# A residual stream turned so that tokens lie on the partitions, in a recurrent and windowed-attention kernel

## The reference, cut to what matters

```python
def ref(x, ...):                                   # x: (8, 256, 128), 8 batches of 256 tokens
    xn = layernorm(x)                              # over the 128 features
    s = recurrence(xn)                             # u = gelu(..)*sigmoid(..); s_t = s_(t-1) A' + u_t B'; y = s C' + D
    h = xn
    for i in range(6):
        h = attn_layer(shift_tokens(h), ...) + h   # q, k, v of 16 heads of 64; l2norm, rotary, window 32, softmax, @ Wo
        h = ffn_layer(shift_tokens(h), ...) + h
    return x + s * silu(h)

def shift_tokens(t):                               # half of the features come from the token before
    a, s = jnp.split(t, 2, -1)
    s = jnp.pad(s, ((0, 0), (1, 0), (0, 0)))[:, :-1]
    return jnp.concatenate([a, s], -1)

def ffn_layer(x, g, bln, W1, b1, W2, b2):
    mu = x.mean(-1, keepdims=True)
    var = ((x - mu) ** 2).mean(-1, keepdims=True)
    xn = (x - mu) / jnp.sqrt(var + 1e-05) * g + bln
    a, gate = jnp.split(xn @ W1 + b1, 2, -1)       # 341 columns each
    return a * jax.nn.gelu(gate, approximate=False) @ W2 + b2
```

## Time and profile before

| | |
|---|---|
| median of 3 runs | 1746.93 us (1746.70 to 1748.54) |
| profiled execution | 1748.49 us, span 1746.7 us |
| PE busy | 1695.2 us (97%), 30558 matmuls |
| PEld | 1198.8 us (69%) |
| DVE | 1391.6 us (80%) |
| ACT | 1232.3 us (71%) |
| POOL | 1129.3 us (65%) |
| share of PE in the chain that ended last | 94% |
| mean granted TensorE clock | 0.991 |

### The profile page before, as it was taken

One profiled execution on the slowest core, in us unless ns is written; L12 is line 12 of the kernel. 1 busy time (PEld: TensorE's weight loads), 2 busy tenths in 40 slices (PEclk: granted clock), 3 DMA queues, 4 the chain that ended last, 5 costly groups with the idle time before them and its releaser, 6 DMA issues.

```text
span 1746.7 us, 72189 instructions
## 1 busy us (share of the span) xinstructions
PE 1695.2 (97%) x30558; PEld 1198.8 (69%) x30558; DVE 1391.6 (80%) x2607; ACT 1232.3 (71%) x2173; POOL 1129.3 (65%) x1066
## 2 busy tenths in 40 slices
PE   5889999999999999999999999999999999999996
PEld 2356777777777777777777777777777777777774
DVE  4688888888888888888888888888888888888762
ACT  2256777777777677777777777777777777777763
POOL 0477676667766766776676676667766666776640
PEclk9799999999999999999999999999999999999998
DMA  3133223323222332222323322322322332322222
GB/s 106 24 93 69 61 57 75 84 70 71 66 59 73 86 75 59 71 61 61 89 66 80 71 60 60 86 70 71 77 63 56 75 88 70 71 63 59 59 56 73
DMA packets 82830, 121.45 MB, mean 70 GB/s; under 512 B 25168, under 2 KB 28752, under 8 KB 82256
## 3 DMA queue, kind: packets, MB, share of 16 engines
q1 hardware_dynamic: 82512, 116.84, 27.8%
HBM read 20.28 MB, written 2.10 MB: 13 GB/s over the span
## 4 chain that ended last, share of the span: by engine, by line
PE 94%; DVE 3%; ACT 2%; issue 1%; DMA 0%; SPq 0%; POOL 0%; DVEq 0%; POOLq 0%; ACTq 0%
PE QKb L452 20%; PE O L543 12%; PE F L525 11%; PE S L452 9%; PE VTb L475 9%; PE S L501 9%; PE S L513 5%; PE F L598 4%; PE F L553 4%; PE F L599 3%; PE S L494 2%; PE F L568 2%; PE F L587 1%; DVE t L833 1%; PE F L560 1%
## 5 line engine op out<-in xcount | busy, mean ns | idle before, releaser
L833 DVE TENSOR_TENSOR t<-QKb,table 128x1024 f32<-128x1024 f32 x384 | 469.3, 1222 | 191.2 <-ACT sq L648 190.9
L977 POOL TENSOR_TENSOR t<-t 128x512 f32<-128x512 f32 x384 | 488.1, 1271 | 202.1 <-DVE t L833 201.1
L956 POOL TENSOR_TENSOR t<-t,rn 128x512 f32<-128x512 f32 x384 | 401.0, 1045 | 163.7 <-DVE rn L880 163.7
L648 ACT ACTIVATE sq<-QKb 128x512 f32<-128x512 f32 x384 | 229.3, 597 | 377.6 <-PE QKb L452 377.6
L452 PE MATMUL QKb<-wq_sb,x_sh 128*128 128x512 f32 x768 | 412.4, 619 | 11.2 <-DVE t L833 10.6
L475 PEld LDWEIGHTS VTb<-cst,t 128*128 128x128 f32 x1536 | 191.9, 141 | 200.2 <-issue 199.0
L842 DVE TENSOR_REDUCE ss<-sq 128x16 f32<-128x1024 f32 x192 | 232.0, 1208 | 0.0
L475 PE MATMUL VTb<-cst,t 128*128 128x128 f32 x1536 | 230.7, 273 | 0.0
L543 PEld LDWEIGHTS O<-PT,V 64*64 64x64 f32 x12288 | 196.7, 135 | 48.2 <-issue 42.4
L543 PE MATMUL O<-PT,V 64*64 64x32 f32 x12288 | 218.0, 221 | 0.4 <-DVE rn L880 0.4
L963 POOL TENSOR_TENSOR E<-E,rs 128x512 f32<-128x512 f32 x192 | 200.0, 1042 | 14.8 <-DVE rs L889 14.7
(11 more groups left out here) (137 smaller groups left out, 2464.2 us busy)
## 6 DMA issues: line engine op xcount, KB each, us to landing
V<-v_tok SPq DMA_DIRECT2D x1440, 64.0 KB, 2.0
wq_sb<-in_wqkv SPq DMA_DIRECT2D x36, 256.0 KB, 3.0
wo_sb<-in_wo SPq DMA_DIRECT2D x6, 512.0 KB, 4.3
w_sb<-in_w SPq DMA_DIRECT2D x6, 341.0 KB, 3.3
w_sb<-in_w SPq DMA_DIRECT2D x6, 192.0 KB, 3.0
y_spill<-OT SPq DMA_DIRECT2D x1, 1024.0 KB, 4.2
V<-y_spill SPq DMA_DIRECT2D x1, 1024.0 KB, 8.3
out<-V SPq DMA_DIRECT2D x4, 256.0 KB, 2.9
```

Source lines behind the costliest of these rows:

```text
L648: act.activation(sq[:, v % 4, :], QK_ps, ACT.Square).then_inc(sq_done, 1)
L833: dve.tensor_tensor(t12[:, v, :, :].rearrange("p c (h d) -> p c h d", h=8), QK_ps.rearrange("p (h d) -> p h d", h=8).unsqueeze(1) .to_broa ...
L956: pool.tensor_tensor(w, w, rn[:, vv // 4, 8 * (vv % 4):8 * (vv % 4 + 1)].unsqueeze(2) .to_broadcast([P, 8, DH]), ALU.mult).then_inc(qk_nor ...
L977: pool.tensor_tensor(w, w, t12[:, v, 1, :].rearrange("p (h c d) -> p h c d", h=8, c=2)[:, :, ::-1, :], ALU.add).then_inc(add_done, 1)
```

## The change

The residual stream becomes `xt[P, B, NT, D]`: 128 tokens on the partitions, two token tiles, features along the free axis. So the output projection and W2 are turned (the activations are stationary, the weights move with 128 columns, one product per token tile). The feed-forward's token shift becomes three transfers from SyncE, from `xm` to `xs`. The statistics are taken along the free axis by VectorE (`bn_stats`, `bn_aggr`), GpSimd adds epsilon, raises to -1/2 and normalises both tiles, TensorE transposes the normalised tiles, and ScalarE applies g and b on the way out of PSUM. W2's bias moves into a spare row of W2, against a row of ones in `hid`. The batch to be staged is transposed by TensorE first (slot `TX`). The reloaded recurrence result is transposed inside the loop (`Y_BACK`), and the end goes batch by batch. Several distances and the order of blocks within a slot change on each engine.

```diff
+Y_BACK = STEPS * SLOTS + 19
-F_WO, F_MID, F_MEAN, F_CENT, F_SQ, F_VAR, F_VCOPY, F_DIAG = 20, 25, 26, 27, 27, 27, 28, 27
-F_BC, F_XN, F_AFF, F_W1, F_GEL, F_HID, F_W2, F_END = 28, 30, 31, 33, 33, 34, 35, 36
+F_WO, F_MID, F_SH, F_ST, F_NM, F_XT, F_AFF = 21, 24, 24, 27, 27, 29, 29
+F_W1, F_GEL, F_HID, F_W2, F_END = 32, 32, 33, 35, 37
+TX = 6
```

On SyncE:

```diff
+                    f, pr = batch(s, par, v, F_SH)
+                    if f is not None:
+                        wait(sp, mid_done, f + 1)
+                        wait(sp, normed, f * NT)
+                        sp.dma_start(xs[:, :, 0:D // 2], xm[:, pr, :, 0:D // 2]).then_inc(xs_moved, 16)
+                        sp.dma_start(xs[1:P, :, D // 2:D], xm[0:P - 1, pr, :, D // 2:D]).then_inc(xs_moved, 16)
+                        sp.dma_start(xs[0:1, 1:NT, D // 2:D], xm[P - 1:P, pr, 0:NT - 1, D // 2:D]).then_inc(xs_moved, 16)
...
+            sp.wait_ge(y_saved, 16)
             sp.wait_ge(o_ready, QUADS)
+            sp.dma_start(y_back, y_spill).then_inc(in_y, 16)
             sp.dma_start(x_tok, x.rearrange("b (t p) d -> p (b t) d", p=P)).then_inc(in_x2, 16)
```

On TensorE:

```diff
+                            for h in (2 * k, 2 * k + 1):
+                                for t in range(NT):
+                                    mm = pe.matmul(BANK_WO[:, D * t:D * (t + 1)], OT[:, pr, h, P * t:P * (t + 1)],
+                                                   wo_sb[:, h, :], start=(h == 0 and t == 0), stop=(h == HP - 1),
+                                                   skip_group_check=True)
...
+                    if v == TX and live(s + 1, STEPS):
+                        wait(pe, ff_final, s + 2 - B)
+                        wait(pe, ff_final, begun(s, v, F_W2))
+                        wait(pe, xn_done, begun(s, v, F_XT))
+                        for t in range(NT):
+                            mm = pe.transpose(BANK_TX[:, P * t:P * (t + 1)], xt[:, (s + 1) % B, t, :], ident)
+                        mm.then_inc(tx_ready, 1)
...
+                    f, pr = batch(s, par, v, F_XT)
+                    if f is not None:
+                        wait(pe, normed, (f + 1) * NT)
+                        wait(pe, ff_final, f)
+                        wait(pe, x_staged, staged(s, v))
+                        for t in range(NT):
+                            mm = pe.transpose(BANK_XT[:, P * t:P * (t + 1)], xn[:, t, :], ident)
+                        mm.then_inc(xnT_ready, 1)
...
+                    if s * SLOTS + v == Y_BACK:
+                        wait(pe, in_y, 16)
...
+                        for t in range(TILES):
+                            mm = pe.transpose(banks[t // 4][:, P * (t % 4):P * (t % 4 + 1)],
+                                              y_back[:, t // NT, P * (t % NT):P * (t % NT + 1)], ident)
+                        mm.then_inc(yT_ready, 1)
...
-                        for r_ in range(NCH):
-                            mm = pe.matmul(BANK_W2[:, 0:N], w2_sb[:, r_, :], hid[:, r_, :],
-                                           start=(r_ == 0), stop=(r_ == NCH - 1))
+                        for t in range(NT):
+                            for r_ in range(NCH):
+                                mm = pe.matmul(BANK_W2[:, D * t:D * (t + 1)], hid[:, r_, P * t:P * (t + 1)], w2_sb[:, r_, :],
+                                               start=(r_ == 0), stop=(r_ == NCH - 1))
                         mm.then_inc(w2_ready, 1)
-                    f, pr = batch(s, par, v, F_VAR)
-                    if f is not None:
-                        wait(pe, xq_done, f + 1)
-                        for t in range(NT):
-                            mm = pe.matmul(BANK_VAR[:, t:t + 1], xq[:, P * t:P * (t + 1)], mean_w[:, 0:1],
-                                           start=True, stop=True)
...
-                        pe.matmul(BANK_BC[:, 0:N], ones[:, :], diag[:, :, :].rearrange("p t q -> p (t q)"),
-                                  start=True, stop=True).then_inc(bc_ready, 1)
...
-                        pe.matmul(BANK_MEAN[:, 0:N], mean_w[:, :], xs[:, :], start=True, stop=True)\
-                          .then_inc(mean_ready, 1)
```

On ScalarE:

```diff
-                        wait(act, xr_done, f + 1)
-                        act.activation(xc[:, :], xc[:, :], ACT.Identity, bias=prm[:, R_B:R_B + 1],
+                        wait(act, xnT_ready, f + 1)
+                        wait(act, w1_ready, f * NCH)
+                        act.activation(xc[:, :], BANK_XT[:, 0:N], ACT.Identity, bias=prm[:, R_B:R_B + 1],
```

On VectorE:

```diff
+                    f, pr = batch(s, par, v, F_ST)
+                    if f is not None:
+                        wait(dve, xs_moved, 48 * (f + 1))
+                        for t in range(NT):
+                            dve.bn_stats(ln6[:, t, :], xs[:, t, :]).then_inc(ln6_done, 1)
+                        wait(dve, normed, f * NT)
+                        for t in range(NT):
+                            wait(dve, ln6_done, f * NT + t + 1)
+                            dve.bn_aggr(ln2[:, t, :], ln6[:, t, :]).then_inc(ln2_done, 1)
...
+            for b in range(B):
+                dve.wait_ge(g_done, b + 1)
+                y_ = banks[b // 2][:, N * (b % 2):N * (b % 2 + 1)].rearrange("p (t d) -> p t d", t=NT)
+                dve.tensor_tensor(xt[:, b, :, :], y_, xt[:, b, :, :], ALU.mult).then_inc(prod_done, 1)
+                dve.wait_ge(prod_done, b + 1)
+                dve.tensor_tensor(o_tok[:, NT * b:NT * (b + 1), :], xt[:, b, :, :], x_tok[:, NT * b:NT * (b + 1), :],
+                                  ALU.add).then_inc(o_done, 1)
```

On GpSimd:

```diff
+                        wait(pool, ln2_done, (f + 1) * NT)
+                        pool.tensor_tensor(rstd[:, :], ln2[:, :, 1], eps2[:, :], ALU.add).then_inc(rstd_done, 1)
+                        wait(pool, rstd_done, 2 * f + 1)
+                        pool.tensor_tensor(rstd[:, :], rstd[:, :], minus_half[:, :], ALU.pow).then_inc(rstd_done, 1)
...
+                            pool.tensor_scalar(xn[:, t, :], xs[:, t, :], ln2[:, t, 0:1], rstd[:, t:t + 1], ALU.subtract, ALU.mult)\
+                                .then_inc(normed, 1)
```

More of the change, by code:

```diff
@@ L55 @@
 C_ALL = C_TAB + 4 * NT * DH
[L57 to L58 removed]
+R_G, R_B, R_B1A, R_B1G = 0, 1, 2, 2 + NCH
+R_ALL = 2 + 2 * NCH
 def live(unit, count):
@@ L106, in s_units, with begun, staged @@
     return upto(s * QPS + (v - L_S) // 2 + 1, QUADS)
+def begun(s, v, lag):
+    return upto(s + (v - lag) // SLOTS + 1, STEPS)
+def staged(s, v):
+    return 2 * (min(s + (v - TX) // SLOTS + 1, STEPS - 1) + 1)
 def upto(count, most):
@@ L638, in _ @@
             act.wait_ge(xT_done, 4)
-            act.wait_ge(set_pool, 4)
-            stage(0, 0)
+            act.wait_ge(set_pool, 5)
+            stage(xf[:, 0:N], 0)
             def step(s, par, b_):
@@ L679, in step @@
                         act.copy(v_tok[:, c // 2, 512 * (c % 2):512 * (c % 2 + 1)], V_ps).then_inc(v_evac, 1)
+                    f, pr = batch(s, par, v, F_GEL)
+                    if f is not None:
+                        gelus(f, pr, [0, 1])
+                    if v == TX and live(s + 1, STEPS):
+                        wait(act, tx_ready, s + 1)
+                        wait(act, qk_ready, s * SLOTS)
+                        wait(act, v_ready, s * (SLOTS // 2))
+                        stage(BANK_TX[:, 0:N], 1 - par)
                     a, k, st, pr = quad(s, par, v, L_PT)
@@ L684, in step @@
                         act.copy(PT[:, k % 2, :, :].rearrange("p c q -> p (c q)"), PT_ps).then_inc(pt_evac, 1)
+                    f, pr = batch(s, par, v, F_HID)
+                    if f is not None:
+                        gelus(f, pr, [2])
                     f, pr = batch(s, par, v, F_AFF)
@@ L705, in step @@
                         act.copy(OT[:, pr, 2 * k:2 * k + 2, :], O2[:, :, 0:N]).then_inc(o_evac, 1)
-                    f, pr = batch(s, par, v, F_GEL)
-                    if f is not None:
-                        gelus(f, pr, [0, 1])
             def gelus(f, par, chunks):
@@ L791, in step @@
                     g = s * SLOTS + v
+                    f, pr = batch(s, par, v, F_W2)
+                    if f is not None:
+                        hidden(f, pr, [2])
                     recurrence(in_fill(s, v, 0))
+                    f, pr = batch(s, par, v, F_MID)
+                    if f is not None:
+                        wait(dve, wo_ready, f + 1)
+                        dve.tensor_tensor(xm[:, pr, :, :], BANK_WO[:, 0:N].rearrange("p (t d) -> p t d", t=NT), xt[:, f % B, :, :],
+                                          ALU.add).then_inc(mid_done, 1)
+                    f, pr = batch(s, par, v, F_END)
+                    if f is not None:
+                        finish(f, pr)
                     f, pr = batch(s, par, v, F_HID)
@@ L837, in step @@
                                           ALU.mult).then_inc(t12_done, 1)
[L839 to L844 removed]
+                    recurrence(in_fill(s, v, 1))
                     a, k, st, pr = quad(s, par, v, L_S)
```

283 lines of the change are left out of this document (101 added, 182 removed).

## The result

| | before | changed |
|---|---|---|
| median (lowest to highest, runs) | 1747.03 us (1746.64 to 1749.63, 8) | 1741.09 us (1736.21 to 1742.79, 8) |
| ratio | 1 | 0.9959 (95% interval 0.9947 to 0.9971) |
| span of the profiled execution | 1746.7 us | 1740.2 us |
| stream of 43 steps (first projection of step 4 to that of step 47) | 1469.3 us | 1463.0 us |
| median step | 34.16 us | 33.36 us |

The account below looks back on a forecast made before the run. TensorE's matmul stream, without holes from step 4 to the last, was taken as the bound. Stream -30.2, release +2.2, drain and end +3.7 made -24.3 us, so 1723 us; the 8-in-10 range was 1708 to 1747.

Parts of the forecast that it names:

- TensorE's stream: TensorE's matmuls per step: three products removed, four transposes added, output projection and W2 turned; net -0.67 us, 30.2 us off.
- 0.05 for a release: Slots 1 and 2: TensorE's next projection waits for VectorE's table multiply; 0.05 us a step, 2.2 us lost.
- rival B: TensorE's 128-column passes are paced by their weight loads; at 0.19 us a pass 158 us more, 1881; chance 0.03.
- rival D: Slot 3 gains 0.1 to 0.2 us, the first four steps a microsecond each: 1712 us; chance 0.15.
- the 0.11 that was kept back: Of the reciprocal-deviation spreading's 0.54 us, 0.11 for standing behind small tiles passes to what stands there next; 0.43 comes off.
- VectorE: Work per step about even, 0.8 us out for 0.9 in; slots 1 and 2 take 7.19 us with no room left.
- ScalarE: One pair of table switches a step goes, with the square and two shifted copies; worth nothing in the full stream.
- GpSimd: Diagonal (613 ns) goes; a small add and two normalising operations, 0.3 us each, not longer than 613 ns, come; zero effect.
- SyncE: Three more transfers per step behind the slot 0 residual sum, some 2.2 us of issue; zero unless landing takes over four times as long.
- rival C: The token shift's transfers land late and VectorE stands in slot 3; one late microsecond gives 1767 us; chance 0.07.
- Drain: Behind the stream: scale-and-bias 4.7 us later by the reload, end +1.3, a 2.31 us TensorE hole goes; net +3.7 us.
- rival A: VectorE becomes the bound, from slots 1 to 4; with 0.5 us a step 1743 us; chance 0.20.

Follow-up runs that it names:

- the two kernels that mend it: Changed kernel with parameters double-buffered and loaded 36 slots earlier: 1718.28 us; changed kernel with W1, W2 and parameter loads two slots earlier, parameters first: 1720.48 us.
- its two variants: Old kernel with the next layer's W1, W2 and parameter loads two slots later: 1783.68 us; old kernel with the mean product issued twice: 1764.28 us.

## Why the prediction was wrong

**TensorE's stream: right.** -0.67 us a step and 0.05 for a release were forecast, and the step is 0.80 shorter. The 128-column passes are 0.111 us apart over the whole kernel, so rival B is out, and with it the Trainium skill's rule (TensorE: Matmul & The Clock Gate, The mechanism) as far as it would have a full-array weight load stand in the stream. The step is 0.2 us shorter still than forecast, and only 0.1 of that is as rival D had it: slot 3 takes 3.94 us where it took 4.26, but the variance product, which was counted, had alone taken 0.36 there, and only the scores became cheaper by themselves (0.89 us to 0.79). The rest is in what stands behind small tiles. By median spacing of starts the four parts of the output projection took 3.86 us and take 3.56, -0.30 where +0.08 was counted, since each part had paid some 0.1 for standing behind the small tiles; the projections and the transposes of `PT`, which stand there now, take 0.39 more, and the 0.11 that was kept back for them is part of this. The 4 us that D saw in the first steps did not come.

What this heading lacked is a term for stalls: the stream was taken to stay full, and the stalls in slot 3 cost 6.6 us in the trace. No view of the old kernel showed one.

**VectorE: right.** Slots 1 and 2 take 7.26 us against the 7.19 worked out, with 0.08 of room: the table multiply of slot 2 ends at 924.10, the next projection starts at 924.18.

**ScalarE: right.** One pair of table loads a step went, and ScalarE is busy for 970 us of the stretch where it was for 1097; in the full stream that is worth nothing, as the step's length shows. ScalarE's order of instructions is what mattered, below.

**GpSimd: sizes off, no effect.** The two normalising operations were put at 0.3 each and "not longer than the 613". From the groups by line of the changed kernel:

```profile
L979 POOL TENSOR_SCALAR xn<-xs,ln,rstd 128x128 f32<-128x128 f32 x96 | 75.5, 795 | 5.0
```

So each took 0.80, and the bound was wrong too; the transposes behind them show no wait.

**SyncE: the step that failed.** Under this heading the prediction counted three transfers, their issue, and whom they hold up, and ended with "Zero". It gave the move of the scale and bias, two slots forward, no term at all. It never asked what else that instruction reads, and where the writer of that stands: the layer's parameters, whose load did not move forward with it, but one slot back. In a steady step there is no such load, and every view that the stream's part of the sum was made from shows a steady step. It was worth 20.9 us in the trace and 20.6 to 22.8 by the medians of the two kernels that mend it (20 to 21 by their ratios to the old kernel run beside each). With it mended, the whole change is worth 27 to 29 us, where the sum had 24.3. The whole of the miss: the steady step gave 6.6 us more than the 28.0 that were counted, the drain 4.6 more, and the layer changes took 20.9, slot 3 8.3, the time before the stream 0.7 (in the trace, whose span is 6.5 us shorter; 0.6 is left over).

A size was off here too, without effect in steady steps. The third transfer moves 64 elements, and costs SyncE far more to issue than the first of 64 KB:

```profile
1709.31 0.67 SPq L384 DMA_DIRECT2D xs<-xm  x1
...
1710.02 0.72 SPq L385 DMA_DIRECT2D xs<-xm  x1
...
1710.78 2.70 SPq L386 DMA_DIRECT2D xs<-xm  x1
```

4.2 us for the three, where 2.2 were counted. VectorE's statistics waited for these transfers once in the whole trace, for 1.7 us, so rival C is out.

**Drain: +3.7 forecast, -0.9 came.** The last middle residual sum began 9.75 us earlier (1718.60 in the earlier trace rows, 1708.85 now), of which 5.6 is the shorter stream. The reload did make the hole that was foreseen, though of 5.8 us, as it landed 5.0 us after its issue and not 8.3; the page's row of the transfer, then the timeline:

```profile
V<-y_spill SPq DMA_DIRECT2D x1, 1024.0 KB, 5.0
```

```profile
1708.85 0.42 DVE L809 TENSOR_TENSOR xm<-F,xt 128x256 f32<-128x256 f32 x1 [6.32 <-PE F L499]
...
1713.58 0.53 SPq L405 DMA_DIRECT2D V<-y_spill  x1
...
1718.63 1.97 PE L607 MATMUL S<-cst,V 128*128 128x128 f32 x8 [5.81 <-DMA V<-y_spill]
...
1724.51 0.56 ACT L713 ACTIVATE xc<-F,prm 128x256 f32<-128x256 f32 x1 [11.19 <-PE F L568]
...
1731.16 0.42 DVE L904 TENSOR_TENSOR xt<-F,xm 128x256 f32<-128x256 f32 x1 [1.70 <-PE F L616]
```

From the middle residual sum to the scale and bias it is 15.7 us, where the earlier trace rows had 10.4: +5.3, near the foreseen +4.7. What the forecast lacked lies on both sides of it. That residual sum comes 4.1 us earlier than the stream alone would bring it; the hole of the earlier trace rows, forecast to go, is still 1.58 us, TensorE's idle pieces of over 0.3 us up to there are 3.1 us in all where they were 4.5, and what brought the rest was not followed. From the scale and bias to the last sum it is 6.7 us where it was 8.7. The tail behind the last sum is 9.0 us as before; +1.3 was forecast. Together -4.1 + 5.3 - 2.0 = -0.8.

**The range.** It held the time (1708 to 1747), by rival A's width and not by its mechanism, so that is luck. (A's own term, 0.5 us in each of 44 steps, is 22 us and not the 20 written there.) The case "a load once per layer is late" was not among the rivals.

## What to carry to other kernels

When an instruction is moved forward, list all that it reads, and for each the place where it is written, in the steps that differ as well: a new layer, the first, the last. A steady step prices the work, and the seldom steps decide whether the price holds. And where a queue also carries bulk traffic, count in its order what stands ahead of a load: here seven moves that took 5.3 us to issue, and held it for 3.3 us after the sum that it waits for was done.

## What the runs showed of the hardware that was not expected

- A stand of TensorE of 2.57 us was followed by a 4 us stretch with a granted clock of 0.61, and one of 6.34 us by a projection with a recorded length of 2.08 us in place of 1.02: the stall's own length is not its whole price.
- A transfer of 64 elements from one partition to another takes 2.6 to 3.2 us to issue (48 times, median 2.72); one of 64 KB over 128 partitions 0.67.
- A tensor-scalar operation on GpSimd with two scalars per partition takes 0.80 us for 128 elements, more than a tensor-tensor multiply of 256 before (0.61).
- TensorE stopped inside a group of matmuls without a semaphore, at the same instruction in different kernels, for 0.2 to 1.8 us, and went on 2.24 to 2.87 us after a 16 KB transfer of instructions began, in all 40 cases. The longest waits came where that transfer began behind the start of a 512 KB load. Why the old kernel and its two variants show none of it stays open.
- Such a stall has its price behind it as well: after one of 1.58 us in slot 3 of step 42 the granted clock was 0.50 from 1474 to 1476 us, and that slot was 2.89 us longer than its median.
